# A fused conditioning, expert and adapter kernel on one core: wait order, the adapter-bias product, gathers and the last tile's stores moved

## The chip, the cores and the metric

One core of a Trainium2 chip runs the whole program. The metric is the device time of one execution in microseconds (us), the median over several runs.

## The reference

The input `x` has 128 samples of 32 rows with 256 columns: 4096 tokens of width 256. Each sample has an index `itok` from 0 to 7. What is computed, cut to what matters:

```
w   = L0_cond_weights[itok]                       # a 32x32 mix of each sample's rows
z   = einsum('bct,bcd->bdt', x, w)                # 4096 tokens x 256
logits = z @ Wg + bg; top 2 of 4 experts, softmax over the two
for each expert: the 1024 tokens with the highest score (capacity)
    y = gelu(tok @ W1) @ W2 * p;  out[token] += y
x1  = x + out
gate, up = x1 @ Wg + lora, x1 @ Wu + lora         # lora: rank 16, chosen by itok
h   = silu(gate) * up;  d = h @ Wd + lora
out = x1 + d @ (weight * scale).T + bias
```

## The kernel before, in words

All engines run their own written-out instruction stream and meet in semaphores. Products of f32 data are made of three products of a high and a low part (lines 1429 to 1431, helper `product`): ScalarE (ACT) writes the high part, VectorE (DVE) the difference.

**The head, 0 to 61 us.** TensorE (PE) makes the expert logits; DVE searches each expert's threshold. Meanwhile PE works through 37 items: 32 mix products of tokens (`item`, line 1482), four products that fold the last weight matrix into `Wd` (`fold_half`, L1496), and one, `item(ITEMS - 1)`, that folds it into the adapter matrix (L1485, the bias product of the title); ACT copies each out. The mixed rows go to `flat_rows` in HBM (queue of SyncE, SP). `route_read` (DVE, to L1086) writes the list of token rows of an expert, `slot_row`, and raises `route_out`; GpSimd (POOL) then gathers the rows: `gather(b)` waits and issues four indirect DMAs of 128 rows (L496). Before `gather(0)` POOL waits for `flat_out` and `spare_out`, that is for the rows in HBM.

**Layer 0, 61 to 250 us.** Eight batches `b` of 512 tokens, two for each expert. A step `s` is one slice of 128 hidden units: PE makes the up product of step s, then the down product of step s - 2 (`down`). Batch 0 and batch 7 are cut into two parts of 256 tokens, with eight steps each, so there are 80 steps. The first batch's four chunks of 128 tokens are transposed by PE (`first_transposed`, L1558): chunks 0 and 1 before step 0, chunk 2 after step 1 and chunk 3 after step 2; ACT copies them out (`first_hi`, L624) and DVE makes the low part (`first_lo`, L1096). `slot_scales(0)` (ACT, L635) follows the last chunk, and `gather(1)` waits for it. Between the chunks and step 0, `keep_busy` runs two products without use (L1527). Chunks 2 and 3 are first needed in step 8. Step 0 begins with four products of high parts of the chunks (L1574) and goes on with two of the low parts (L1577).

In the first half the order of PE's stream is: `first_transposed(0)`, `item(ITEMS - 1)`, `first_transposed(1)`, a wait for the copy of that item, `keep_busy`, a wait for the low parts of `w1`, step 0.

**Between the layers, 237 to 263 us.** Layer 1 sorts the samples into eight tiles of 16, each with at most two adapters. POOL's order there is: `scatter(6)`; `gather_b(0)` and `gather_b(1)`, which load the adapter matrices of tiles 0 and 1 (L531, 128 rows of 8 KB each, so 1 MB each); a wait for `ids_in` (from DVE, L1202, the tokens' order) and three more semaphores; four gathers of the first tile's rows (`x1_first`, L561, 128 KB each); a wait until they have landed; `scatter(7)`. PE waits for the four (`first_in`) and transposes them (L1638) between the down products of the last two steps.

**Layer 1, 263 to 587 us.** Eight tiles of 512 tokens in eight steps each. The last tile's output is finished in two halves of 256 tokens: PE ends a half (L1733 to 1735), DVE adds bias and residual with one instruction for each of two column blocks (`finish_last`, L1368), and `last_stores` (L390) writes it: 16 samples, one DMA of 32 KB each, eight on SP's queue and eight on ACT's, four for each half. A store of 32 KB is 256 pieces of 128 bytes (2 blocks x 128 partitions x 32 numbers). Earlier tiles are stored by SP alone (L474).

Of the kernel before, what the change touches and what calls it, by code (L numbers as in the profile page):

```python
# [63 lines left out]
def adaln_moe_lora(nc, A, outT):  # L64
# [11 lines left out]
    with ctx:  # L76
# [247 lines left out]
        out_done = [sem(f"out_done{i}") for i in range(2)]  # L324
# [47 lines left out]
        FIRST_BANKS = (6, 7, 4, 5)  # L372
        LO_W1, LO_ALL = 2 * KD, 2 * KD + 2
# [7 lines left out]
        def last_stores(queue, side):  # L381

            t, n = NB1 - 1, SB // 4
            mine = [[(2 * j + side) * n + i for i in range(n)] for j in range(2)]
            to = [[queue.value_load(sample_at[0:1, t * SB + i:t * SB + i + 1], min_val=0, max_val=TOK // 32 - 1) for i in half]
                  for half in mine]
            for j in range(2):
                queue.wait_ge(out_ev, KD * (NB1 + j))
                for i, s_ in zip(mine[j], to[j]):
                    queue.dma_start(out_v[:, :, bass.ds(s_, 1), :], out_sb[1][:, :, i * 32:(i + 1) * 32].unsqueeze(2)  # L390
                                    ).then_inc(out_done[1], 16)
# [4 lines left out]
        def _(sp):  # L396
# [79 lines left out]
            last_stores(sp, 0)  # L476
            sp.wait_ge(out_done[0], 16 * SB * NB1 // 2)
            sp.wait_ge(out_done[1], 16 * SB * NB1 // 2)

        @block.gpsimd  # L480
        def _(pool):
# [7 lines left out]
            def gather(b):  # L489
                e, half = b // 2, b % 2  # L490
                pool.wait_ge(route_out, e + 1)
                if b:
                    pool.wait_ge(xsT, parts_before(b))
                    pool.wait_ge(slot_in, b)
# [21 lines left out]
            pool.wait_ge(flat_out, 128)  # L516
            pool.wait_ge(spare_out, 32)
# [36 lines left out]
            for t in range(2):  # L554
                gather_b(t)
# [4 lines left out]
            for q in range(GB):  # L560
                pool.indirect_dma_start(  # L561
                    out=x1_first[:, q, :], out_offset=None, in_=x1_rows[:, :],
                    in_offset=bass.IndirectOffsetOnAxis(ap=x1_row[:, q:q + 1], axis=0)).then_inc(first_in, 16)
            pool.wait_ge(first_in, 16 * GB)
# [5 lines left out]
            for t in range(2, NB1):  # L570
                gather_x1(t)
                gather_b(t)
                gather_bd(t)

        @block.scalar
        def _(act):
# [92 lines left out]
            first_hi(0)  # L669
            act.wait_ge(item_mm, ITEMS)  # L670
            act.activation(raw_bd[:, 0, :], bank[(ITEMS - 1) % 4][:, 0:D], ACT.Copy).then_inc(item_ev, 1)
            first_hi(1)
            for s in range(STEPS0):
# [8 lines left out]
                if s in (1, 2):  # L682
                    first_hi(s + 1)
                if s == 2:
# [97 lines left out]
            last_stores(act, 1)  # L782

        @block.vector
        def _(dve):
# [451 lines left out]
            for s in range(STEPS0):  # L1237
# [4 lines left out]
                if s in (1, 2):  # L1242
                    first_lo(s + 1)
# [645 lines left out]
```

## Time and profile before

| | us |
|---|---|
| median of 3 runs | 589.03 (589.01 to 590.47) |
| time of the profiled execution | 588.83 |
| its span | 587.0 |
| PE busy | 562.7 (96%) |
| DVE busy | 372.0 (63%) |
| ACT busy | 242.4 (41%) |
| POOL busy | 142.6 (24%) |

The span runs from the first to the last record of the profile; 1.8 us of the execution's time lie around it. An engine's busy time counts its instructions alone, and the ends of matmuls are modelled.

### The profile page before, as it was taken

To read this page: it belongs to the slowest core of one execution; us is meant where nothing else is said; L and a number is where in the kernel's file an instruction comes from. 1 tells how busy PE (TensorE), PEld (TensorE's weight loads), DVE (VectorE), ACT (ScalarE), POOL (GpSimd) and SP (SyncE) were. 2 spreads that over 40 slices of the span, in tenths; PEclk is the share of its full clock that TensorE was granted. 3 is DMA by queue.
4 is the path that set the end of the run, shared out by engine and by line. 5 is a ranking of instruction groups with operands and counts; after the bars stand their busy time and mean duration, and the time that the engine had idled before them with its cause. 6 is when DMAs were issued, how large, how long until landed. Compare 5 with 4: busy or idle time off the path is not lost.

```text
span 587.0 us, 10367 instructions
## 1 busy us (share of the span) xinstructions
PE 562.7 (96%) x3583; PEld 470.0 (80%) x3583; DVE 372.0 (63%) x901; ACT 242.4 (41%) x545; POOL 142.6 (24%) x122
## 2 busy tenths in 40 slices
PE   4778999999999999999999999999999999999996
PEld 3556899999999999978878878788788788787885
DVE  7989668656776567665574575575665645754733
ACT  2645558747766655653322322324124123123110
POOL 3001402657446442664012030030030030100000
PEclk9999999999999999999999999999999999999999
DMA  8994666884285231732004022041041040120012
GB/s 327 340 358 164 205 237 187 228 186 68 53 229 169 46 46 17 201 54 73 0 10 135 10 93 59 3 129 25 0 135 17 0 141 11 64 59 5 12 26 36
DMA packets 64798, 61.04 MB, mean 104 GB/s; under 512 B 37456, under 2 KB 56656, under 8 KB 63472
## 3 DMA queue, kind: packets, MB, share of 16 engines
q1 hardware_dynamic: 53312, 37.97, 21.3%
q0 software_dynamic: 9264, 22.22, 15.5%
q10 hardware_dynamic: 2176, 0.26, 0.3%
q8 instruction: 25, 0.41, 0.3%
q14 instruction: 21, 0.17, 0.1%
HBM read 45.17 MB, written 19.47 MB: 110 GB/s over the span
## 4 chain that ended last, share of the span: by engine, by line
PE 89%; DVE 5%; DMA 3%; POOL 1%; issue 1%; SPq 0%; ACT 0%; DVEq 0%; POOLq 0%
PE bank L1429 25%; PE bank L1431 24%; PE bank L1430 24%; PE bank L1698 5%; PE bank L1656 3%; DMA xT<-in_xT 1%; DMA x_first<-x_rows,x_row 1%; PE bank L1536 1%; DMA xg<-flat_rows,slot_row 1%; PE bank L1545 1%; PE bank L1648 1%; PE bank L1445 1%; PE bank L1665 1%; PE bank L1666 1%; PE bank L1786 1%
## 5 line engine op out<-in xcount | busy, mean ns | idle before, releaser
L760 ACT ACTIVATE act<-bank 128x512 f32<-128x512 f32 x64 | 38.2, 598 | 183.0 <-PE bank L1698 183.0
L1385 DVE TENSOR_TENSOR prod<-bank,act 128x512 f32<-128x512 f32 x64 | 44.2, 690 | 97.7 <-PE bank L1698 97.3
L1241 DVE TENSOR_TENSOR hid_lo<-hf,hid_hi 128x512 fp32r<-128x512 f32 (+1 forms) x80 | 46.6, 585 | 52.9 <-ACT hf L681 52.4
L1429 PE MATMUL bank<-w_hi,hid_hi 128*128 128x256 f32 x256 | 71.8, 280 | 0.0
L1430 PE MATMUL bank<-w_lo,hid_hi 128*128 128x256 f32 x256 | 71.4, 279 | 0.0
L1431 PE MATMUL bank<-w_hi,hid_lo 128*128 128x256 f32 x256 | 71.3, 279 | 0.0
L678 ACT ACTIVATE hid_hi<-bank 128x512 fp32r<-128x512 f32 (+1 forms) x80 | 41.1, 514 | 64.8 <-PE bank L1431 63.3
L507 POOL DMA_INDIRECT x_rows<-y_sb,slot_row x32 | 52.1, 1628 | 42.5 <-ACT y_sb L648 24.6
L531 POOL DMA_INDIRECT b_pair<-b_rows,b_row x8 | 8.2, 1028 | 200.7 <-PE bank L1746 200.0
L1429 PE MATMUL bank<-xs_hi,w_hi 128*128 128x512 f32 (+1 forms) x158 | 56.5, 357 | 0.0
L1431 PE MATMUL bank<-xs_hi,w_lo 128*128 128x512 f32 (+1 forms) x158 | 55.0, 348 | 0.0
L496 POOL DMA_INDIRECT xg<-flat_rows,slot_row x32 | 35.3, 1103 | 80.4 <-DVE slot_row L1086 33.2
L1430 PE MATMUL bank<-xs_lo,w_hi 128*128 128x512 f32 (+1 forms) x158 | 54.8, 347 | 0.0
L1429 PE MATMUL bank<-hid_hi,wd_hi 128*128 128x512 f32 (+1 forms) x144 | 52.7, 366 | 0.0
L1431 PE MATMUL bank<-hid_hi,wd_lo 128*128 128x512 f32 (+1 forms) x144 | 52.7, 366 | 0.0
L1430 PE MATMUL bank<-hid_lo,wd_hi 128*128 128x512 f32 (+1 forms) x144 | 52.6, 365 | 0.0
L1429 PE MATMUL bank<-x1s_hi,wg_hi 128*128 128x512 f32 x124 | 50.4, 407 | 0.0
L1430 PEld LDWEIGHTS bank<-w_lo,hid_hi 128*128 128x128 f32 x256 | 48.2, 188 | 2.0
L1429 PEld LDWEIGHTS bank<-w_hi,hid_hi 128*128 128x128 f32 x256 | 48.1, 188 | 2.0
L1430 PE MATMUL bank<-x1s_lo,wg_hi 128*128 128x512 f32 x124 | 48.7, 393 | 0.0
L1431 PE MATMUL bank<-x1s_hi,wg_lo 128*128 128x512 f32 x124 | 48.4, 390 | 0.0
L1431 PE MATMUL bank<-x1s_hi,wu_lo 128*128 128x512 f32 x124 | 48.4, 390 | 0.0
(323 smaller groups left out, 1258.6 us busy)
## 6 DMA issues: line engine op xcount, KB each, us to landing
w_raw<-in_L_ffn_W SPq DMA_DIRECT2D x8, 1024.0 KB, 6.9
flat_rows<-x_sb SPq DMA_DIRECT2D x8, 520.0 KB, 5.3
x_sb<-in_x SPq DMA_DIRECT2D x8, 512.0 KB, 8.7
x_rows<-in_x SPq DMA_DIRECT2D x4, 1024.0 KB, 8.6
outT<-out_sb SPq DMA_DIRECT2D x120, 32.0 KB, 1.6
xT<-in_xT SPq DMA_DIRECT2D x3, 1024.0 KB, 7.4
xT<-in_xT SPq DMA_DIRECT2D x2, 512.0 KB, 10.6
wdT<-in_wdT SPq DMA_DIRECT2D x1, 1024.0 KB, 6.0
```

Of the source, the lines that this page charges most:

```text
L496: pool.indirect_dma_start(out=xg[:, q, :], out_offset=None, in_=flat_rows[:, :], in_offset=bass.IndirectOffsetOnAxis(ap=slot_row[:, e, hal ...
L507: pool.indirect_dma_start(out=x1_rows[:, :], out_offset=bass.IndirectOffsetOnAxis(ap=slot_row[:, e, half * GB + q:half * GB + q + 1], axis=0),
L531: pool.indirect_dma_start(out=b_pair[t % 2][:, :].bitcast(f32), out_offset=None, in_=b_rows[:, :], in_offset=bass.IndirectOffsetOnAxis(ap= ...
L678: act.activation(hid[s % 4][0][:, n], bank[s % 2][:, n], ACT.Gelu)
L760: act.activation(act1[h % 2][:, :], bank[h % 2][:, :], ACT.Silu).then_inc(silu1, 1)
L1241: dve.tensor_tensor(lo[:, n], hf[s % 2][:, n], hi[:, n].bitcast(f32), ALU.subtract).then_inc(hid0, 1)
L1385: dve.tensor_tensor(prod[par][h][:, :], bank[2 + h % 2][:, :], act1[h % 2][:, :], ALU.mult).then_inc(prod1, 1)
L1429: pe.matmul(out, lh, rh, start=start, stop=False, skip_group_check=True)
L1430: pe.matmul(out, lh, rl, start=False, stop=False, skip_group_check=True)
L1431: return pe.matmul(out, ll, rh, start=False, stop=stop, skip_group_check=True)
L1656: last = pe.matmul(bank[6][r, :], ad_pair[par][:, h, :], prod[par][h][:, :], start=h < 4, stop=h >= 4, skip_group_check=True, tile_positio ...
L1698: pe.matmul(out[:, :], b_pair[par][:, i * HID + h * P:i * HID + (h + 1) * P], u[:, :], start=False, stop=True, skip_group_check=True).then ...
```

## The change

Five edits:

1. POOL: the waits for `flat_out` and `spare_out` stand inside `gather(0)`, behind the one for `route_out`.
2. PE: `item(ITEMS - 1)` comes ahead of `first_transposed(0)`, and `keep_busy` between `first_transposed(0)` and `first_transposed(1)`, behind a wait for the items up to the last but one. ACT copies that item out ahead of `first_hi(0)`.
3. Chunk 3 is transposed, copied and split after step 3, not after step 2 (`LATE_STEPS`), and `slot_scales(0)` goes with it.
4. POOL: `gather_b(1)` is issued after the four gathers of the first tile's rows.
5. The last tile: samples 6 and 7 are stored by POOL on a semaphore of its own; SP and ACT store seven each. DVE makes the additions of the second half in two lots of 128 tokens (four instructions of 128 columns for two of 256), and each queue waits for the lot it stores. SP waits for POOL's stores too at the end.

```diff
+        LATE_STEPS = (1, 3)
...
-            t, n = NB1 - 1, SB // 4
-            mine = [[(2 * j + side) * n + i for i in range(n)] for j in range(2)]
...
+        LAST_SP, LAST_ACT, LAST_POOL = (0, 1, 2, 8, 9, 12, 13), (3, 4, 5, 10, 11, 14, 15), (6, 7)
+        def last_stores(queue, mine, landed):
+            t, seen = NB1 - 1, None
+            to = [queue.value_load(sample_at[0:1, t * SB + i:t * SB + i + 1], min_val=0, max_val=TOK // 32 - 1) for i in mine]
+            for i, s_ in zip(mine, to):
+                lots = 0 if i < 8 else 1 + (i - 8) // 4
+                if lots != seen:
+                    queue.wait_ge(out_ev, KD * (NB1 + lots))
+                seen = lots
+                queue.dma_start(out_v[:, :, bass.ds(s_, 1), :], out_sb[1][:, :, i * 32:(i + 1) * 32].unsqueeze(2)
+                                ).then_inc(landed, 16)
...
-            last_stores(sp, 0)
+            last_stores(sp, LAST_SP, out_done[1])
             sp.wait_ge(out_done[0], 16 * SB * NB1 // 2)
-            sp.wait_ge(out_done[1], 16 * SB * NB1 // 2)
+            sp.wait_ge(out_done[1], 16 * (SB * NB1 // 2 - len(LAST_POOL)))
+            sp.wait_ge(pool_out, 16 * len(LAST_POOL))
...
             def gather(b):
                 pool.wait_ge(route_out, e + 1)
+                if b == 0:
+                    pool.wait_ge(flat_out, 128)
+                    pool.wait_ge(spare_out, 32)
...
-            pool.wait_ge(flat_out, 128)
-            pool.wait_ge(spare_out, 32)
             gather(0)
...
-            for t in range(2):
-                gather_b(t)
+            gather_b(0)
             pool.wait_ge(ids_in, 4)
...
+            gather_b(1)
             pool.wait_ge(first_in, 16 * GB)
             scatter(NB0 - 1)
...
+            last_stores(pool, LAST_POOL, pool_out)
...
-            first_hi(0)
             act.wait_ge(item_mm, ITEMS)
             act.activation(raw_bd[:, 0, :], bank[(ITEMS - 1) % 4][:, 0:D], ACT.Copy).then_inc(item_ev, 1)
+            first_hi(0)
             first_hi(1)
...
-                if s in (1, 2):
-                    first_hi(s + 1)
-                if s == 2:
+                if s in LATE_STEPS:
+                    first_hi(2 + LATE_STEPS.index(s))
+                if s == LATE_STEPS[1]:
                     slot_scales(0)
...
-                    for k in range(KD):
-                        dve.wait_ge(acc1, NB1 + (KD if j else k))
-                        dve.scalar_tensor_tensor(out_sb[1][:, k, c], last_out(j, k), out_bias[:, k:k + 1],
-                                                 x1T[1][:, k, c], ALU.add, ALU.add).then_inc(out_ev, 1)
+                    for at_ in range(0, BT // 2, P) if j else (0,):
+                        n = P if j else BT // 2
+                        to = slice(c.start + at_, c.start + at_ + n)
+                        for k in range(KD):
+                            dve.wait_ge(acc1, NB1 + (KD if j else k))
+                            dve.scalar_tensor_tensor(out_sb[1][:, k, to], last_out(j, k)[:, at_:at_ + n], out_bias[:, k:k + 1],
+                                                     x1T[1][:, k, to], ALU.add, ALU.add).then_inc(out_ev, 1)
...
+            item(ITEMS - 1)
             first_transposed(0)
-            item(ITEMS - 1)
+            pe.wait_ge(item_ev, ITEMS - 1)
+            keep_busy(WAIT_ROWS, bank[2], w1)
             first_transposed(1)
             pe.wait_ge(item_ev, ITEMS)
-            keep_busy(WAIT_ROWS, bank[2], w1)
             pe.wait_ge(lo0, LO_W1)
```

DVE's `first_lo` and PE's `first_transposed` in the steps are changed to `LATE_STEPS` in the same way as ACT's `first_hi`.

## Rows read from the trace of the kernel before

**Rows 1.** Waits of PE, whole span: total us, times, longest.
```profile
PE bank L1558 <- DMA xg<-flat_rows,slot_row: 1.3, 2, 1.0
PE bank L1638 <- DMA x_first<-x_rows,x_row: 1.2, 1, 1.2
```
**Rows 2.** Timeline of PE, 59 to 78: start, us, instruction [idle before <-releaser].
```profile
59.32 0.33 PE L1558 MATMUL bank<-ident_r,xg 128*128 128x128 f32 x2 [1.05 <-DMA xg<-flat_rows,slot_row]
59.49 1.10 PE L1485 MATMUL bank<-wfT_s,bdT 128*128 128x256 f32 x4
60.53 0.22 PEld L1558 LDWEIGHTS bank<-ident_r,xg 128*128 128x128 f32 x2 [0.35 <-DMA xg<-flat_rows,slot_row]
61.06 0.74 PE L1527 MATMUL bank<-w_hi 128*128 128x512 f32 x2 [0.16 <-ACT raw_bd L671]
...
62.10 0.40 PE L1577 MATMUL bank<-xs_lo,w_hi 128*128 128x256 f32 x2
...
64.65 0.28 PE L1431 MATMUL bank<-w_hi,hid_lo 128*128 128x256 f32 x1
65.14 0.36 PE L1558 MATMUL bank<-ident_r,xg 128*128 128x128 f32 x2 [0.21 <-DMA xg<-flat_rows,slot_row]
...
77.99 0.45 PE L1545 MATMUL bank<-ident_r,xg 128*128 128x128 f32 x4
```
**Rows 3.** Timeline of POOL, 56 to 88, the first gather of three batches.
```profile
56.25 1.14 POOL L496 DMA_INDIRECT xg<-flat_rows,slot_row  x1 [17.52 <-DVE slot_row L1086]
...
66.80 0.95 POOL L496 DMA_INDIRECT xg<-flat_rows,slot_row  x1 [5.09 <-ACT slot_p L635]
...
87.25 1.16 POOL L496 DMA_INDIRECT xg<-flat_rows,slot_row  x1 [15.72 <-DVE slot_row L1086]
```
**Rows 4.** Timeline of DVE, 55 to 87 and 239: the lists' last instructions and two low parts.
```profile
55.21 0.17 DVE L1086 SCALAR_TENSOR_TENSOR slot_row<-route_t 128x8 int32<-128x8 f32 x1
...
59.55 1.21 DVE L1102 TENSOR_TENSOR w_lo<-w_raw,w_hi 128x1024 fp32r<-128x1024 f32 x1
...
61.35 0.42 DVE L1096 TENSOR_TENSOR xs_lo<-bank,xs_hi 128x256 fp32r<-128x256 f32 x1 [0.26 <-ACT xs_hi L624]
...
86.81 0.17 DVE L1086 SCALAR_TENSOR_TENSOR slot_row<-route_t 128x8 int32<-128x8 f32 x1
...
239.11 1.08 DVE L1202 TENSOR_SCALAR x_row<-bank,pack_f 32x32 int32<-32x32 f32 x4
```
**Rows 5.** Timeline of POOL, 237 to 257: an adapter gather, first tile's gathers, last scatter.
```profile
237.54 1.01 POOL L531 DMA_INDIRECT b_pair<-b_rows,b_row  x1 [0.30 <-issue]
...
240.46 0.95 POOL L561 DMA_INDIRECT x_first<-x_rows,x_row  x1 [0.43 <-DVE x_row L1202]
...
244.41 1.55 POOL L561 DMA_INDIRECT x_first<-x_rows,x_row  x1 [0.30 <-issue]
...
256.26 1.56 POOL L507 DMA_INDIRECT x_rows<-y_sb,slot_row  x1 [0.31 <-issue]
```
**Rows 6.** DMA issues in the window 240 to 241: times, median us to landing.
```profile
x_first<-x_rows,x_row POOLq DMA_INDIRECT x1, 6.1
```
**Rows 7.** DMA issues of the whole span: times, median us to landing.
```profile
x_sb<-x_rows,x_row POOLq DMA_INDIRECT x28, 3.1
```
**Rows 8.** Timeline of PE, 250 us: the transposes of the first tile.
```profile
250.44 0.83 PE L1638 MATMUL bank<-ident_r,x_first 128*128 128x128 f32 x8 [1.24 <-DMA x_first<-x_rows,x_row]
```
**Rows 9.** Timeline, 579 to 585: the last additions and the last stores' issues.
```profile
579.83 0.87 DVE L1368 SCALAR_TENSOR_TENSOR out_sb<-bank,pack_f,x1T 128x256 f32<-128x256 f32 x2
...
580.88 4.26 SPq L390 DMA_DIRECT2D outT<-out_sb  x8
...
580.88 4.38 ACTq L390 DMA_DIRECT2D outT<-out_sb  x8
...
582.02 0.88 DVE L1368 SCALAR_TENSOR_TENSOR out_sb<-bank,pack_f,x1T 128x256 f32<-128x256 f32 x2 [1.32 <-PE bank L1735]
```
**Rows 10.** Stretches: us, PE, PEld, DVE, ACT, POOL busy, clock, DMA share, GB/s.
```profile
584.00:585.00 1.00, 0.00 (x0) 0.00 (x0) 0.00 (x0) 0.00 (x0) 0.00 (x0) 0.72 0.88 130
```

More of the change, by code:

```diff
@@ L323, in adaln_moe_lora @@
         acc1, out_ev = sem("acc1"), sem("out_ev")
-        out_done = [sem(f"out_done{i}") for i in range(2)]
+        out_done, pool_out = [sem(f"out_done{i}") for i in range(2)], sem("pool_out")
         b_out, packed_in, placed, ids_mm, ids_in = (sem("b_out"), sem("packed_in"), sem("placed"), sem("ids_mm"),
@@ L379, in adaln_moe_lora @@
         out_v = outT.rearrange("k p (s n) -> p k s n", n=32)
-        def last_stores(queue, side):
-            t, n = NB1 - 1, SB // 4
-            mine = [[(2 * j + side) * n + i for i in range(n)] for j in range(2)]
[L385 to L391, printed above, removed]
+        LAST_SP, LAST_ACT, LAST_POOL = (0, 1, 2, 8, 9, 12, 13), (3, 4, 5, 10, 11, 14, 15), (6, 7)
[9 more added lines that the diff above has]
+                                ).then_inc(landed, 16)
         block = ctx.enter_context(nc.Block())
@@ L781, in _ @@
             steps1(NB1 - 1, 1, False, True)
-            last_stores(act, 1)
+            last_stores(act, LAST_ACT, out_done[1])
         @block.vector
@@ L1241, in _ @@
                 dve.tensor_tensor(lo[:, n], hf[s % 2][:, n], hi[:, n].bitcast(f32), ALU.subtract).then_inc(hid0, 1)
-                if s in (1, 2):
-                    first_lo(s + 1)
+                if s in LATE_STEPS:
+                    first_lo(2 + LATE_STEPS.index(s))
                 if h in (4, 6) and b + 1 < NB0 and (b or part):
@@ L1619, in _ @@
                     down(s - 2)
-                if s in (1, 2):
-                    first_transposed(s + 1)
+                if s in LATE_STEPS:
+                    first_transposed(2 + LATE_STEPS.index(s))
                 if h in (3, 5) and b + 1 < NB0 and (b or part):
```

## The prediction

> **What bounds it now.** The first thing to read is the page's table of busy time: PE is busy for 562.7 of 587.0 us, so only places where PE stands still, and the tail behind its last product, can give time back. The list of PE's waits over the whole span is read next: behind the head (before 50 us) it has three entries with a DMA or a copy behind them, and two of them hold 2.5 us: the transposes of the first batch's chunks (L1558, 1.3 us in two waits) and those of the first tile (L1638, 1.2 us in one) [rows 1]. From 66 to 249 us and from 263 to 581 us PE waits for nothing. The chain of waits passes through both places: `slot_row`, the four POOL gathers, their DMA; and the tokens' order, four POOL gathers, their DMA. The timelines around the two places and around the end then give the terms.
>
> **The change, part by part.** I count against the profiled execution: span 587.0, time 588.83, which is 0.2 under the median of 589.03.
>
> *POOL's wait order (edit 1).* `slot_row` ends at 55.21 + 0.17 = 55.38 and the first gather starts at 56.25, 0.87 later; in batch 2 the same instruction ends at 86.98 and its gather starts at 87.25, 0.27 later [rows 3, 4]. The rows were stored long before, so no DMA explains the difference. What differs is where the wait for the late semaphore stands: third of three, right before the DMA, in batch 0; first of three, with two satisfied waits behind it, in batch 2. The wait for the tokens' order, first of four, also takes 0.27 (239.11 + 1.08 = 240.19, gather at 240.46) [rows 4, 5]. The edit puts `route_out` first. I take 0.27: the gathers start 0.60 earlier. Bounds: 0 (the position was not the reason) and 0.60.
>
> *Item, keep_busy and the copies (edit 2).* PE is idle from 58.27 to 59.32 and waits again before 60.53 [rows 2]. The four products of the bias item run in the first gap: starts are (60.53 - 59.49)/4, at most 0.26, apart, so from 58.27 to about 59.2. Then comes chunk 0, whose rows landed at about 59.3 [rows 2] and now land 0.6 earlier; then `keep_busy`, at most 0.74; then chunk 1 at about 60.1, its rows having landed at 59.93 (60.53 - 0.60). ACT copies the item ahead of chunk 0's copy; before, that copy ended 0.47 behind the item (60.59 to 61.06), so chunk 0 is held up by less than 0.5, and both chunks' high parts are there before 61.0. Behind that DVE is late next: it makes `w_lo` from 59.55 to 60.76, then chunk 0's low part, then chunk 1's. Its last start was 61.35, after ACT; without that wait it follows chunk 0's at 61.02, 0.34 behind it at the earliest, and ends at 61.02 + 0.42 = 61.44 [rows 4]. So the low products of step 0 start at 61.47 in place of 62.10 [rows 2]: 0.63. If edit 1 gives nothing, chunk 1 stays at 60.53, its low part ends at about 61.75, and the gain is 0.33.
>
> *Chunk 3 a step later (edit 3).* The down product before chunk 3 issues its last matmul at 64.65, the next could go at 64.77, and the transposes start at 65.14: 0.37 of waiting for the fourth gather [rows 2]. One step of batch 0 is 1.4 us, and that wait goes. The two transposes themselves (0.2) only move. ACT's and DVE's copies of the chunk move with them and lie beside PE; they are needed in step 8. `slot_scales(0)` moves too, so `gather(1)` starts some 0.5 us later than 66.80 [rows 3]: one step later (+1.4), less the 1.0 that PE is ahead. Its fourth issue is three times 1.25 behind its first, about 71, and lands some 3 to 4 us later, at 75, against its first use at 77.99 - 1.0 = 77.0 [rows 2, 3]. Cost nothing; two microseconds cover it. SP's queue waits for these rows before it loads the second expert's weights, and those are first used in step 16, five steps behind this place.
>
> Head together: 0.63 + 0.37 = **1.00**, between 0.70 and 1.10.
>
> *Gather_b(1) behind the first tile's gathers (edit 4).* POOL is not the gain: the first `x1_first` gather starts 0.27 after the tokens' order and does so still. What goes is 1 MB in front of these gathers in POOL's queue of transfers. The first of them took 6.1 us from issue to landing [rows 6], where gathers of the same size later take 3.1 [rows 7]. The fourth was issued at 244.41 and PE started at 250.44, after 1.24 of waiting, ready at 249.20 [rows 5, 8]. With 3.1, plus 0.6 for its longer issue (1.55 for 0.95), it lands at 248.1, before PE is ready, and all of the wait goes: 1.24. But the last gather of a group has landed late before: the first batch's fourth, issued some 4.5 behind 56.25, held PE until 65.14, 4.3 later, where its first landed in 3.0 [rows 2, 3]. With 4.3 and the 0.6 it lands at 249.3, and 1.1 is left. I take **1.10**. Lower bound 0, if the late landing has nothing to do with the queue. `gather_b(1)` itself (1.0 us and 0.3 between issues) now stands ahead of `scatter(7)`, and its semaphore is used 30 us later. The scatter waits for the landing anyway; its first two rows start no later than before (250.57), its last two wait for ACT, and `gather_x1(1)` behind it has 12 us until its first use.
>
> *The last tile (edit 5).* SP's eight issues take 4.26 us, that is seven spacings of 0.556 and a last issue of some 0.37; it starts at 584.77, ACT's last at about 584.86, and the span ends 2.14 after that [rows 9]. The second half's additions end at 582.02 + 0.88 = 582.90 [rows 9], when the four earlier issues end too: queue and DVE are late together. With the change, three issues end at 582.54 at the queue. DVE's lots: an instruction of 256 columns takes 0.44; one of 128 saves half of its columns, about 0.14, so 0.30, and the first lot is there at 582.62, the second at 583.22 (all four cost 1.2, where two cost 0.88). A queue starts 0.18 after DVE (580.70 and 580.88 in the first half) [rows 9]: 582.80, 583.36, then 583.91, 584.47. The last issue starts **0.30** earlier. Upper bound 0.56: one issue less and no wait for DVE.
>
> POOL's two stores start at about 581.0 (0.27 behind the addition) to 581.5 (0.8). The trace before has no store of this kind from POOL. Lower bound 0.95 an issue, as a gather of 128 rows; upper 3.1, twice a scatter of 128 rows (1.56) [rows 5], for 256 pieces. I take 1.0 to 1.5, nearer the gather, a plain copy without addition: the second issue ends at 583.3 to 584.3 and lands 2.2 later, before SP's and ACT's last, at 586.4. They hide it. That cover ends at 1.9 per issue.
>
> A third queue may also move nothing. While the stores run, the DMA engines are 88% busy at 130 GB/s [rows 10]. If that is the limit, the stores end when they did before, and the tail gives 0 where I take 0.30. The Trainium skill says so (DMA: Bandwidth & Descriptors, "Rules for kernel authors"): spreading DMAs over SP, ACT and GpSimd does not help bandwidth, all run on the same 16 engines, and only issue time is saved. The row does not decide it: at 100% the same bytes would still take some 12% less than the 4.2 us they took.
>
> POOL's first gathers of batches 0 and 2 took 1.14 and 1.16, that of batch 1 0.95, with DVE at work beside the longer ones [rows 3]. The Trainium skill (SBUF — State Buffer, "Who interferes with whom") has it that a DVE instruction in a 2-port mode, or with two SBUF inputs, shuts GpSimd out until it ends. By that rule gathers that start 0.6 earlier fall beside other DVE instructions, and one may take up to 0.5 more or less; chunk 1 has half a microsecond of slack against DVE's low parts.
>
> **Sum.** 1.00 + 1.10 + 0.30 = 2.40: span 584.6, profiled time 586.4, median 589.03 - 2.40 = **586.6**. Behind each place PE has no wait for 180 and 320 us, so what is won stays won.
>
> **Rivals.**
> - *The wait's position is not the reason* and the landing tail stays: head 0.70, first tile 0 to 0.5, tail 0.3, so 1.0 to 1.5: 587.5 to 588.0. For it: only one pair of rows with the same instruction. Against: the third case, the tokens' order. Chance 0.18.
> - *The DMA engines bound the last stores*: tail 0, total 2.1: 586.9. Chance 0.15.
> - *POOL's stores come last, slower than before.* Place: behind 580.7 on POOL. Price P for each: the second lands at 581.0 + 2P + 0.3 + 2.2 = 583.5 + 2P, and the other queues' last at 586.4. At 1.9 (twice a gather) it lands at 587.3, 0.6 after the old landing at about 586.7; the total is 1.5: 587.5. At 3.1 it lands at 589.7; 3.0 lost less 2.1 won: 589.9, slower. The sign turns at P = 2.65. For it: 256 pieces, and POOL's work is by row. Against: a gather of 8 KB rows takes POOL 1.01, hardly more than one of 1 KB (0.95) [rows 5]. Chance 0.12 for 1.9 and about, 0.05 for over 2.65.
> - *A gain is given back*, by batch 1's rows or the second expert's weights being late at 77 to 90 us, up to 1.0: 587.6. Two microseconds of slack are against it. Chance 0.05.
>
> That leaves 0.45 for the forecast, 586.6, whose own range is 586.0 to 587.1 (head 0.9 to 1.1, first tile 0.95 to 1.24, tail 0.1 to 0.56). The range for 8 in 10 reaches to the rivals on the fast side of no change and takes in the upper bounds: 585.8 to 588.2.
>
> A measurement of this kernel can tell about 0.3%, 1.8 us, from no change, which puts the line at 587.26. Below it lie the forecast, the engine-bound rival and a little of the others: 0.66. Between: the wait rival, POOL at 1.9, given back: 0.29. Slower by over 0.3% needs POOL's stores above 3.5 us each or something unseen: 0.05.
>
> **What would show it.** The first gather starts 0.27 after `slot_row`; the wait for chunk 3 is gone and step 4 is 1.0 earlier; `x1_first`'s first gather lands in about 4 us, not 6.1, and PE's wait at L1638 is under 0.3; the last issues of SP and ACT start some 2.4 us earlier than 584.8 and POOL's second store lands before theirs. I am wrong if POOL still takes 0.87, if L1638 still waits a microsecond, or if the chain's end is a POOL store.

## The result, and the profile after

The changed kernel takes 593.07 us (median of six executions, 591.80 to 594.13) where the kernel before takes 589.09 beside it: a ratio of 1.0066, 95% interval 1.0050 to 1.0082. It is **slower by 4.0 us**; the prediction was 586.6, faster by 2.4.

The profiled execution took 593.32, its span is 591.6, 4.6 over the 587.0 of before. The page's head, chain and busy times:

```profile
span 591.6 us, 10371 instructions
PE 564.7 (95%) x3583; PEld 472.1 (80%) x3583; DVE 372.7 (63%) x903; ACT 242.0 (41%) x545; POOL 143.1 (24%) x124
PE 90%; DVE 5%; DMA 2%; issue 1%; ACT 0%; SPq 0%; POOL 0%; POOLq 0%; ACTq 0%; DVEq 0%
```

PE's work is no less, and the chain no longer goes through gathers (DMA 2% for 3%). The list of PE's waits, those behind 56 us, answers to [rows 1] (line numbers moved with the edits: L1567 is the L1558 of before, the transposes of the first batch's chunks):

```profile
PE bank L1438 <- ACT hf L687: 1.2, 1, 1.2
...
PE bank L1567 <- DMA xg<-flat_rows,slot_row: 0.7, 1, 0.7
PE bank L1584 <- ACT xs_hi L630: 0.6, 1, 0.6
...
PE bank L1438 <- DVE hid_lo L1247: 0.3, 1, 0.3
```

The wait for `x_first` is gone, as forecast. In its place stands one of the same size for ACT, a little earlier in time. The timeline of POOL after (for [rows 3] and [rows 5]) shows the edits doing what they say:

```profile
57.69 1.18 POOL L503 DMA_INDIRECT xg<-flat_rows,slot_row  x1 [18.91 <-DVE slot_row L1092]
59.16 1.50 POOL L503 DMA_INDIRECT xg<-flat_rows,slot_row  x1 [0.30 <-issue]
...
242.07 0.97 POOL L565 DMA_INDIRECT x_first<-x_rows,x_row  x1 [1.90 <-DVE x_row L1208]
...
247.54 0.94 POOL L536 DMA_INDIRECT b_pair<-b_rows,b_row  x1 [0.30 <-issue]
```

`slot_row` ends at 57.40 here, so the gather follows it by 0.29, where it was 0.87. But the second gather takes 1.50; in the kernel before it took 0.97:

```profile
57.70 0.97 POOL L496 DMA_INDIRECT xg<-flat_rows,slot_row  x1 [0.30 <-issue]
```

The end of the run is where the time is. Three views of after: POOL's timeline, the engines' last instructions (source line L76, the closing of the block; columns: shortest, median and longest duration in ns, then the first and the last start in us), and SP's waits.

```profile
584.38 1.52 POOL L393 DMA_DIRECT2D outT<-out_sb  x2 [69.56 <-issue]
```

```profile
L76 POOLq DRAIN  x1: 6405/6405/6405, 585.0 to 585.0; - x1
L76 ACTq DRAIN  x1: 150/150/150, 587.3 to 587.3; - x1
L76 SPq COMPARE_BRANCH  x1: 41/41/41, 589.0 to 589.0; - x1
L76 SPq EVENT_SEMAPHORE  x1: 17/17/17, 591.5 to 591.5; - x1
```

```profile
SPq L76 <- PEq L76: 2.3, 1, 2.3
```

All stores have landed and SP is through its waits at 589.0. DRAIN is the instruction with which each engine closes its stream. POOL's runs from 585.0 to 591.4, and the program ends 0.2 behind it. (The wait is written down as one for PE's sequencer, but PE had long been done; the row to read is the DRAIN.) In the kernel before the same instruction was out of sight in the middle of the last tiles, behind POOL's last DMA:

```profile
511.60 0.95 POOL L539 DMA_INDIRECT bd_pair<-bd_rows,bd_row  x1 [0.30 <-issue]
```

```profile
L76 POOLq DRAIN  x1: 12964/12964/12964, 508.9 to 508.9; - x1
L76 SPq COMPARE_BRANCH  x1: 41/41/41, 586.6 to 586.6; - x1
```

It ended at 521.8 there, 9.3 after that DMA's issue had ended, and nobody waited for it.

**Four distances.** To compare executions I cut each span at three events: `slot_row`'s end; the start of step 0's low products (62.10 in [rows 2]); the end of PE's last product; the end of the span. For after against before they give

| | before | after | difference |
|---|---|---|---|
| start to `slot_row` | 55.38 | 57.40 | +2.02 |
| to step 0's low products | 6.72 | 6.57 | -0.15 |
| to the end of the last product | 519.89 | 520.29 | +0.40 |
| to the end of the span | 5.01 | 7.34 | +2.33 |
| sum | 587.0 | 591.6 | +4.60 |

The first line lies wholly ahead of the change. PE's sixteen logit products took 2.02 us before and 3.42 after, and the stretches 16:20 and 20:24 (columns as in [rows 10]) say why. Before, then after:

```profile
16.00:20.00 4.00, 2.59 (x28) 2.06 (x18) 3.36 (x12) 2.65 (x4) 1.03 (x1) 1.00 1.09 353
20.00:24.00 4.00, 3.15 (x15) 2.72 (x15) 3.76 (x29) 3.33 (x9) 0.00 (x0) 1.00 1.09 353
```

```profile
16.00:20.00 4.00, 2.59 (x28) 1.96 (x27) 3.57 (x12) 2.10 (x3) 1.04 (x1) 0.88 1.09 353
20.00:24.00 4.00, 4.00 (x19) 3.73 (x19) 1.89 (x14) 2.93 (x7) 0.00 (x0) 0.70 1.09 352
```

The granted clock was full, 2.4 GHz, throughout before, and for a part of these 8 us at its lower level, 1.2 GHz, in after. PE had been busy for all of 12:16 in after (4.00) and for 3.92 of it in before.

### The profile page after: what moved, and what is told of

It reads as the page before. It is cut to its first block, busy times and chain, and to the rows that moved or that the text cites. A ratio compares the mean times of both kernels' runs of the same rounds, so it can differ in the third digit from the quotient of the medians.

```text
span 591.6 us, 10371 instructions
## 1 busy us (share of the span) xinstructions
PE 564.7 (95%) x3583; PEld 472.1 (80%) x3583; DVE 372.7 (63%) x903; ACT 242.0 (41%) x545; POOL 143.1 (24%) x124
## 4 chain that ended last, share of the span: by engine, by line
PE 90%; DVE 5%; DMA 2%; issue 1%; ACT 0%; SPq 0%; POOL 0%; POOLq 0%; ACTq 0%; DVEq 0%
PE bank L1438 25%; PE bank L1440 24%; PE bank L1439 24%; PE bank L1708 5%; PE bank L1666 3%; DMA xT<-in_xT 1%; DVE passed L887 1%; PE bank L1454 1%; PE bank L1545 1%; PE bank L1554 1%; PE bank L1658 1%; PE bank L1675 1%; PE bank L1676 1%; PE bank L1796 1%; PE bank L1517 1%
```

## The experiments

Theory A: POOL's DRAIN behind its late stores makes the tail 2.3 longer. Rivals: B, the stores' landing or the smaller lots of the last additions; C, the middle (ACT's stand-still) belongs to edit 4; D, the late `slot_row` belongs to the edits. The kernel before was timed beside all of them, and each ratio is against it.

### 1. The last tile alone, and the change without POOL's stores

`b_only_tail` is the kernel before with edit 5. `a_no_pool_stores` is the kernel after with this edit, cut (SP's waits at the end are changed to match):

```diff
-LAST_SP, LAST_ACT, LAST_POOL = (0, 1, 2, 8, 9, 12, 13), (3, 4, 5, 10, 11, 14, 15), (6, 7)
+LAST_SP, LAST_ACT = (0, 1, 2, 3, 8, 9, 12, 13), (4, 5, 6, 7, 10, 11, 14, 15)
...
-            last_stores(pool, LAST_POOL, pool_out)
```

> The kernel before with edit 5 alone (the last tile: POOL stores two samples, seven each on SP and ACT, last additions in two lots). Theory A, from the trace after: two DMAs late on POOL's queue put POOL's closing DRAIN behind them, and it ends about 5.5 us after the last of them is issued, where SP's own end would come 0.3 earlier than before or at the same time. So this kernel is 2.0 to 2.6 us slower than before (about 591.3), with the chain ending in POOL's DRAIN near the span's end. Rival B, the prediction's own step: the tail gives 0 to 0.3 (588.7 to 589.1), and the time of after is lost in the head and the middle. Head and middle (to 580 us) should stand within 0.5 us of the kernel before by either.

> The kernel after, but POOL stores nothing and SP and ACT have eight stores each again (the two lots of the last additions stay). Theory A: 2.3 us less than after, 590.8. Rival B (the lots, or the landing of the stores, hold the end): within 0.5 us of after.

Measured: `b_only_tail` 592.05, ratio 1.0061 (1.0044 to 1.0079); `a_no_pool_stores` 587.21, ratio 0.9987 (0.9973 to 1.0000), both beside 588.53. The last product ends at 581.95 in the first and at 580.99 in the second; their spans, 589.3 and 586.0, end 7.35 and 5.01 behind it. Theory A stands, and the lots of the last additions are worth nothing: 5.01 with them, 5.01 without. The second kernel came out 3.6 under the expected 590.8, which had been counted from 593.07, the first measurement of after; section 5 shows what else was in that one. The chain of `b_only_tail` is as follows (start, us, what):

```profile
580.82 1.24 issue
582.05 0.04 POOLq L392
582.10 0.06 POOL outT L392
582.16 0.52 issue
582.67 0.93 POOLq L76
```

```profile
L76 POOLq DRAIN  x1: 6402/6402/6402, 582.7 to 582.7; - x1
L76 ACTq DRAIN  x1: 150/150/150, 585.0 to 585.0; - x1
L76 SPq COMPARE_BRANCH  x1: 41/41/41, 586.7 to 586.7; - x1
```

The seven stores did what was forecast for the issue and nothing for the end. SP's issues end at 584.80 (580.84 + 3.96), 0.34 before the 585.14 of [rows 9], with the last product at the same time (581.95 against 581.99). SP is through its waits at 586.7; before, at 586.6. The DMA engines' busy share falls to 0.27 in the half microsecond from 585.95, after 0.97 and 0.95 in the two ahead of it; in the kernel before it falls to 0.15 in that from 585.99. The same bytes end at the same time.

The median is 3.5 over before, though, not 2.3. Experiment 3 finds 0.45 of the rest.

### 2. One store of POOL, early or late, and stores out of the way

`b_pool_one_first_half` and `b_pool_one_second_half` are the kernel before, with POOL taking sample 7, or sample 15, from ACT (cut; the line for sample 15 has `NB1 + 1`, and SP's waits at the end are changed to match):

```diff
...
+            pool.wait_ge(out_ev, KD * (NB1 + 0))
+            pool.dma_start(out_v[:, :, bass.ds(s_, 1), :], out_sb[1][:, :, i * 32:(i + 1) * 32].unsqueeze(2)).then_inc(pool_out, 16)
```

`b_pool_stores_tile6` is the kernel before with two stores on POOL, samples 6 and 7 of the last tile but one (tile 6), taken from SP.

> The kernel before, but POOL stores one sample of the last tile, in its first half (one for the two of edit 5; ACT has seven, SP eight). Theory A1 (DRAIN ends a fixed 5.5 us after POOL's last issue has ended): the store is issued at about 582.1 to 582.9, DRAIN ends at 588.4, the span is 1.4 over that of before. Theory A2 (DRAIN is a fixed 6.4 us from where it starts): it starts at about 582.2, ends at 588.6, and the span is 1.6 over. Rival B (nothing of DRAIN depends on the stores): no change.

> The kernel before, but POOL stores one sample of the last tile's second half (sample 15, from ACT). Theory A: the store can be issued 2.2 later than in the first half; it took 1.4 from the addition's end to its start and 0.78 itself, and DRAIN ended 5.4 after it in three profiles. The second half's additions end 0.9 after PE's last product and a bit, so DRAIN ends at 0.95 + 1.4 + 0.8 + 5.4 = 8.6 behind PE's last product, where the kernel before ends 5.0 behind it: 3.6 slower (about 592.1). A rival in which late stores cost by their landing alone (2.2 to 2.4 after the issue): 0 to 0.6 slower.

> The kernel before, but POOL stores two samples of tile 6, some 25 us before the end, in place of SP. Theory A (only the place of POOL's last DMA counts, its DRAIN needs 5 to 6 us after it and is hidden here): the time of before within 0.3, DRAIN over by 570 us. Rival E (the mere use of direct stores on POOL costs something, in the code of POOL or in its first gathers, whose first took 1.17 to 1.18 in both profiles with such stores and 1.14 in all four without): 0.5 to 1.2 slower than before, with the first gather at 1.17 and the second at 1.48.

| | ratio (interval) | span's end behind the last product |
|---|---|---|
| one store, first half | 1.0034 (1.0020 to 1.0048) | 6.50 |
| one store, second half | 1.0077 (1.0052 to 1.0101) | 8.69 |
| two stores, tile 6 | 1.0007 (0.9990 to 1.0023) | 5.05 |

POOL's stores and DRAIN, first of the second-half kernel, then of the tile-6 kernel:

```profile
583.71 0.78 POOL L580 DMA_DIRECT2D outT<-out_sb  x1 [71.75 <-issue]
```

```profile
L76 POOLq DRAIN  x1: 6193/6193/6193, 583.7 to 583.7; - x1
L76 SPq COMPARE_BRANCH  x1: 41/41/41, 586.2 to 586.2; - x1
```

```profile
553.13 1.52 POOL L581 DMA_DIRECT2D outT<-out_sb  x2 [39.93 <-issue]
```

```profile
L76 POOLq DRAIN  x1: 6402/6402/6402, 553.7 to 553.7; - x1
```

The later store moves the end with it: it starts 2.30 behind the last product, where the early one starts 0.12 behind, and the ends are 2.19 apart. SP is ready 3.7 before DRAIN is over. DRAIN ended at 589.3 for an issue that ended at 583.9 (583.12 + 0.78), 589.9 for 584.5, 560.1 for 554.65, and 589.1 for 583.60 in `b_only_tail`: **5.4 to 5.5 us behind the end of POOL's last direct issue**, whether one or two (the other five kernels or repeats with such stores give the same), and out of sight where 27 us follow. One store less saved 0.85 (7.35 to 6.50), one issue. That is theory A1; A2's fixed 6.4 fails, as DRAIN took 6.19 with one store and 6.40 with two. The tail of the first-half kernel is 1.5 longer than before's and its median 2.1 over, again more than the tail.

### 3. What direct stores on POOL do to the head

All kernels with a direct store on POOL, tile 6 among them, have another head: rival E had forecast gathers of 1.17 and 1.48 for the tile-6 kernel, and they took 1.17 and 1.48, while its 0.5 in the time lies within the interval. The gathers of the first batch in the tile-6 kernel with edits 1 to 4 (`edits_1_to_4_pool_tile6`), and those of edits 1 to 3 alone:

```profile
57.59 1.17 POOL L503 DMA_INDIRECT xg<-flat_rows,slot_row  x1 [19.33 <-DVE slot_row L1097]
59.06 1.50 POOL L503 DMA_INDIRECT xg<-flat_rows,slot_row  x1 [0.30 <-issue]
```

```profile
56.12 1.14 POOL L500 DMA_INDIRECT xg<-flat_rows,slot_row  x1 [17.53 <-DVE slot_row L1088]
57.57 0.97 POOL L500 DMA_INDIRECT xg<-flat_rows,slot_row  x1 [0.30 <-issue]
```

> Edits 1 to 4, the last tile as before, and POOL stores two samples of tile 6. Theory F (any direct store on POOL makes its first gathers slower, also here): gathers of 1.17, 1.5, 1.45, low products of step 0 at 6.6 after slot_row in place of 6.12, end of the span 5.0 behind PE's last product, DRAIN hidden; the time 0.5 over edits 1 to 4. Theory G (the slower gathers belong to the place of the stores at the end): 6.12 and the time of edits 1 to 4.

Measured: 590.90, ratio 1.0016 (0.9998 to 1.0034), beside 1.0010 for edits 1 to 4 in the same measurement; low products of step 0 at 6.55, the tail 5.07, DRAIN hidden. That is theory F in the trace; a time difference of 0.4 is within the intervals. Over all twenty traces, the second gather took 1.47 to 1.50 in the ten with a direct store on POOL and 0.97 in the ten without. Step 0's low products, measured from `slot_row`:

| | without a direct store on POOL | with |
|---|---|---|
| no edit in the head | 6.72, 6.76, 6.76 | 7.24, 7.18, 7.11, 7.19 |
| edits 1 to 3 | 6.12, 6.12, 6.12, 6.11, 6.11 | 6.57, 6.66, 6.59, 6.55, 6.59, 6.55 |

So edits 1 to 3 give 0.6 in either column, and the stores take 0.45 back, 520 us before they run. The first gather is 0.03 longer there, and the second then lies otherwise against DVE's four `w_lo` instructions beside it. That this shift makes the step of 0.5 is likely (gathers took 0.95 to 0.97, 1.43 to 1.50 or 1.98 to 2.02 in this place, in jumps of half a microsecond) but wasn't tried. For it speaks that in the ten traces with such stores a `w_lo` instruction had begun 0.05 to 0.09 ahead of the second gather and took 0.68 to 0.69, while in the ten without it had begun 0.02 to 0.04 ahead and took 0.74 to 0.77, and the gather was the short one. Why the first gather is longer is open.

### 4. The head's edits, together and apart

> The kernel before with edits 1 to 3 alone. Theory D1: the 2.0 us by which slot_row comes later after the change is the state of that one execution's clock (granted clock .88 to .90 at 15 to 30 us), not the edits, so this kernel is 0.4 (what the trace after shows between slot_row and 80 us) to 1.0 (the prediction) faster than before, and slot_row ends at about 55.4. Theory D2: the edits shift the code so that the head is slower whenever they are in: slot_row ends near 57.4 and the time is 1.0 to 1.6 over before (590.1 to 590.7).

> The kernel before with edit 1 alone (POOL waits for route_out first). The prediction's step: the first gather starts 0.27 to 0.29 after slot_row where it was 0.87, so chunk 0 comes 0.60 earlier, and the low products of step 0, 6.72 after slot_row before, come 0.2 to 0.6 earlier. Rival (the place of the wait is nothing, the three edits of the head work only together): the gather stays at 0.87 and step 0 at 6.7. In the time at most 0.6 either way, which three rounds can't tell from nothing; the trace tells it.

> The kernel before with edit 2 alone (the bias item ahead of chunk 0, keep_busy ahead of chunk 1). The prediction gives 0.33 where edit 1 gives nothing: the first gather at 0.87 after slot_row, the low products of step 0 at 6.4 after it. Rival: PE only waits elsewhere, 6.7. Edits 1 and 2 with 3 gave 6.12.

| | ratio (interval) | first gather after `slot_row` | low products of step 0 after `slot_row` |
|---|---|---|---|
| edits 1 to 3 | 0.9985 (0.9973 to 0.9998) | 0.29 | 6.12 |
| edit 1 | 0.9992 (0.9979 to 1.0005) | 0.28 | 6.20 |
| edit 2 | 1.0016 (1.0001 to 1.0031) | 0.88 | 6.67 |

Edit 1 alone is 0.52 of the 0.60. Edit 2 alone is 0.05, where 0.33 was expected; its time lies just above that of before, which its trace doesn't explain. Its timeline of PE, and that of edits 1 to 3:

```profile
60.73 0.37 PE L1558 MATMUL bank<-ident_r,xg 128*128 128x128 f32 x2 [0.42 <-DMA xg<-flat_rows,slot_row]
```

```profile
59.56 0.69 PE L1529 MATMUL bank<-w_hi 128*128 128x512 f32 x2
60.38 0.36 PE L1560 MATMUL bank<-ident_r,xg 128*128 128x128 f32 x2
61.31 0.35 PE L1577 MATMUL bank<-xs_hi,w_hi 128*128 128x256 f32 x1 [0.56 <-DVE w_lo L1104]
...
61.95 0.50 PE L1580 MATMUL bank<-xs_lo,w_hi 128*128 128x256 f32 x2
```

With edit 2 alone chunk 1's rows land when they did before, PE waits 0.42 for them, and the copy behind them, which `keep_busy` used to cover, is a wait of 0.56. From chunk 1's transposes to the first high product it is 0.93 in both (61.31 less 60.38; the first high product of edit 2 is at 61.66); before it was 1.10.

Theory D1 holds: `slot_row` ended at 55.83 with edits 1 to 3 and at 57.06 with edit 4 alone, whose head is the code of before, with a granted clock of 0.86 and 0.71 in the two stretches. It is the execution's clock.

### 5. Edit 4, and two kinds of measurement

> The kernel before with edit 4 alone (the second gather of adapter matrices behind the first tile's gathers). Theory C1: the wait of 1.24 before the transposes of the first tile goes, and the 2.2 us in which ACT stood still at 247 to 249 us in the trace after belongs to that execution or to the shifted stream, so this kernel is 1.0 to 1.2 faster than before (588.0). Theory C2: the edit itself makes ACT stand still (the gather of adapter matrices moved beside it), so PE's wait changes its place and the time is that of before or up to 0.7 above (589.1 to 589.8).

> The kernel after, unchanged, once more. The trace after shows 2.3 us lost at the end, slot_row 2.0 late and ACT standing still for 2.2 us at 247 to 249 us. Theory A+random: only the 2.3 is there in every execution; in this profile PE's last product to the end of the span is 7.3 again, while ACT's gap before hid_hi near 249 is 0.7 to 1.0 and slot_row ends anywhere from 55.4 to 57.4; the median is 589.5 to 591.5. Theory S (the change as a whole makes the head late and ACT stand still each time): slot_row again near 57.4, the gap again 2.2, and the median again near 593, 5 over the kernel without POOL's stores.

> The kernel after, unchanged, a third time. It was 1.0066 of before in its first six executions and 1.0029 in the next twelve, beside a kernel before that moved by 0.6 only. Theory J (what came on top of the 2.3 at the end, ACT's stand-still near 248 and the late slot_row, belongs to single executions or to one loading of the program): ratio 1.002 to 1.004, hid_hi's gap near 249 at 0.7 to 1.0, PE's last product 517.9 to 518.1 after step 0's low products. Theory S (it comes back in a part of the executions of this kernel whatever the chip): a ratio near 1.006 again, or executions of both kinds within the twelve.

> The kernel after, unchanged, a fourth time. Theory J (what was on top in the first six executions, ACT's stand-still of 2.2 near 248 us among it, belongs to that loading): 1.002 to 1.005 of before, tail 7.3, PE's last product 517.9 to 518.1 after the low products of step 0. Theory S: 1.006 or more, or PE's last product over 520 after step 0.

Edit 4 alone: 588.68, ratio 1.0001 (0.9990 to 1.0013), no gain. That is theory C2's time without its mechanism, as ACT stands still for 0.7 only in this trace. Yet the trace shows the edit at work: `x_first`'s first gather lands in 2.9 us (6.1 in [rows 6]), PE doesn't wait before the transposes, and the last product comes 518.04 after step 0, 1.85 less than in before.

The kernel after had five measurements. The distance is that from step 0's low products to the end of the last product; the gap is the longest time ACT stood still before `hid_hi` at 246 to 251 us:

| | this / before | ratio (interval) | distance | gap |
|---|---|---|---|---|
| after | 593.07 / 589.09 | 1.0066 (1.0050 to 1.0082) | 520.29 | 2.23 |
| after_again | 590.13 / 588.53 | 1.0029 (1.0017 to 1.0041) | 517.93 | 0.73 |
| after_third | 590.68 / 588.28 | 1.0042 (1.0026 to 1.0058) | 517.95 | 0.72 |
| after_fourth | 593.58 / 590.45 | 1.0060 (1.0036 to 1.0084) | 521.07 | 2.30 |
| after_fifth | 594.68 / 590.15 | 1.0068 (1.0049 to 1.0086) | 521.16 | 2.30 |

The tail was 7.31 to 7.35 in all five. What differs is ACT. The `hid_hi` rows in its timeline, of after and of after_again:

```profile
246.37 0.39 ACT L684 ACTIVATE hid_hi<-bank 128x256 fp32r<-128x256 f32 x1 [0.96 <-PE bank L1440]
...
249.26 0.38 ACT L684 ACTIVATE hid_hi<-bank 128x256 fp32r<-128x256 f32 x1 [2.23 <-PE bank L1440]
```

```profile
246.94 0.38 ACT L684 ACTIVATE hid_hi<-bank 128x256 fp32r<-128x256 f32 x1 [0.73 <-PE bank L1440]
...
249.73 0.38 ACT L684 ACTIVATE hid_hi<-bank 128x256 fp32r<-128x256 f32 x1 [0.71 <-PE bank L1440]
```

By PE's rows the product that the second copy of after reads ended at 248.06 (247.78 + 0.28), 1.2 before the copy started, and PE then stood still for 1.22. In the first measurement of after and in the last two the stand-still is there, in the other two it isn't. Theory J was half right: it doesn't belong to single executions, it comes with the measurement. Theory S is wrong, as two measurements don't have it. A chip of the same number gave one measurement of each kind (after_third, after_fifth), so it isn't simply the chip.

Two more kernels ran beside `after_fourth`: edits 1 to 4 and the change without POOL's stores, each for the second time.

> The kernel before with edits 1 to 4 and the last tile as before. If the lots and the seven stores give nothing (the two profiles with them end 5.0 after PE's last product, as before does), this is the same as the kernel after without POOL's stores: 587.2, 1.3 under before. If the lots help, it is 0.3 above that; if they cost, 0.3 below.

> Edits 1 to 4 once more (0.9990 of before the first time). From the traces: 0.6 at step 0, 0 to 0.3 at chunk 3, and the wait before the first tile's transposes, which was 1.24, 1.16, 1.21 and 0.40 in the four traces without edit 4 and without POOL's stores: together 1.0 to 2.1, so a ratio of 0.9965 to 0.9983. If PE's clock in the head takes it back on average, 0.999 again.

> The kernel after without POOL's stores once more (0.9987 of before the first time). If the lots of the last additions and the order of the stores give nothing, the same as edits 1 to 4 beside it, within 0.4; if they give the 0.30 of the prediction, that much less, which these rounds can't tell from nothing. The tail behind PE's last product is 5.0 either way by the traces so far.

| | first time: ratio, distance | second time: ratio, distance |
|---|---|---|
| edits 1 to 4 | 0.9990 (0.9978 to 1.0002), 518.06 | 1.0010 (0.9996 to 1.0023), 521.48 |
| after without POOL's stores | 0.9987 (0.9973 to 1.0000), 518.04 | 1.0007 (0.9990 to 1.0024), 522.05 |

All four traces of the second measurement have the gap (2.27 to 2.30). There the two kernels' last product comes 3.4 and 4.0 later after step 0 (0.7 of it is another wait for ACT, near 75 us), and what they win elsewhere is gone: `e14_again` came out at 1.0010 where at most 0.9990 was expected. Beside them after was 593.58, 3.2 over the same kernel without POOL's stores, of which the traces show some 2.3 in the tail and 0.44 at step 0 (6.55 to 6.11).

The last pair asked whether the kernel before has the stand-still too.

> The kernel before, unchanged, with a profile of its own. If the kernel after, run beside it, shows ACT's stand-still of 2.2 near 249 us: by theory K (it belongs to the chip) it is here too, and PE's last product comes over 520 us after the low products of step 0; by theory L (edit 4 brings it on such chips) it is not, and the 1.2 of waiting before the first tile's transposes is. If after shows no stand-still on this chip: the wait before the first tile's transposes is 0.4 to 1.24 as in the four traces without edit 4 and without direct stores on POOL, and the low products of step 0 come 6.7 after slot_row.

> The kernel after, unchanged, as the marker of the chip: the tail 7.3 behind PE's last product and the low products of step 0 at 6.6 after slot_row whatever the chip; ratio 1.003 to 1.004 where ACT's gap near 249 us is 0.7, 1.006 where it is 2.2.

`after_fifth` shows it (2.30). `before_again`, beside it, shows a smaller one:

```profile
246.81 0.38 ACT L678 ACTIVATE hid_hi<-bank 128x256 fp32r<-128x256 f32 x1 [1.44 <-PE bank L1431]
```

Its distance is 519.65. In the other measurements the kernels without edit 4 and without direct stores had 519.89, 519.32, 519.36 and 518.76, waits of 1.24, 1.16, 1.21 and 0.40 before the transposes among it; here there is no such wait. So on such a measurement the kernel before loses about what it would have waited anyway, while kernels with edit 4 go from 518.0 to 520.3 to 522.1: neither K nor L alone. The median of before, though, was 589.09, 590.45 and 590.15 in the three measurements with the gap and 588.53, 588.53 and 588.28 in the three without; its one trace there doesn't show where that is lost. I can't tell what holds ACT. In the six traces with a gap of 2.2 or more, a packet of the instruction queue q8 began 0.3 to 0.9 us before the gap's end:

```profile
q8 instruction: 1, 0.02, 11.5%
```

(after, window 248.5 to 249.0; the gap ends at 249.26). Such a packet runs there in the other traces as well, without a gap, no row ties q8 to ACT, and the packet took 0.92 (11.5% of 16 engines for 0.5 us), so it was still under way when ACT went on; it was in the other five too. So this is a weak suspicion. What does go with the gap is an 8 KB packet of the other instruction queue, q14: it came 3.1 to 3.2 behind the gap's end in the six, and 0.2 to 1.2 ahead of the same copy in the thirteen traces in which ACT stood still for 0.7. Whether it is a cause or a consequence isn't shown. The Trainium skill (Runtime: NRT & Kernel Launch, "Instruction fetch mechanics") has each engine fetch its instructions in blocks of 16 KiB by a DMA queue of its own; the packet's 0.02 MB fits one block, and no run here took that transfer away.

## Why the prediction was wrong

**The step that failed is edit 5's, "They hide it".** I followed POOL's two stores to their landing, ahead of 586.4, and no further. Each issue took 0.76 (two in 1.52), less than my 1.0 to 1.5 and far from the 2.65 at which I had the sign turn. The first started 1.40 behind its additions (580.68 to 582.08 in the trace of the tail alone), where I had 0.3 to 0.8. The landing was indeed hidden. What I didn't count is that an engine also has to close: POOL's DRAIN ends 5.4 to 5.5 behind its last direct issue. The term of +0.30 measured -2.3 in the tail and -0.45 in the head, 3.1 off in all, and that alone turns the forecast's -2.4 into +0.7, about half of the way to the measured +4.0. "Slower by over 0.3%" had a chance of 0.05, for very slow stores "or something unseen"; it was the latter, and the chain's end runs through POOL's store and DRAIN, the last of the signs of being wrong. The row was there to be read: the DRAIN of before, 13 us long, ending 9.3 behind POOL's last DMA.

**The rival with the right sign had the wrong price.** "POOL's stores come last" named the place and the side, and gave it 0.05 because it priced the issue alone. Its formula was also misread: 583.5 + 2P reaches the cover's 586.4 at P = 1.45, not at 1.9. With 0.76 to 0.78 an issue that made no difference.

**The rest of edit 5.** The last issue of SP ended 0.34 earlier (0.30 predicted), and the landing did not: the rival of the bound DMA engines was right. The Trainium skill's rule that spreading DMAs over the issuing engines saves issue time and no bandwidth (DMA: Bandwidth & Descriptors, "Rules for kernel authors") is what the runs show: SP through at 586.7 for 586.6. The lots alone did nothing, since a queue with eight stores is behind the additions anyway.

**Edit 1 was right.** The position of the wait gives 0.59 (0.87 to 0.28). Its share at step 0 alone is 0.52.

**Edit 2 was right in the sum and wrong in the parts.** 0.60 for the 0.63 predicted, but edit 2 alone gives 0.05 for my 0.33. I had looked only at DVE's low part, 1.24 behind chunk 1's transposes; PE's own way is longer, 0.93 for the copy and 0.55 for the four high products, with nothing between the transposes and the first of them now. The gathers' 0.5 more beside other DVE instructions, which I had as a possibility with half a microsecond of slack, is what happened in after, and the slack was not there. The rule of the Trainium skill that I weighed there (SBUF — State Buffer, "Who interferes with whom") has a DVE instruction with two SBUF inputs contend only with a GpSimd instruction that reads SBUF, a condition that I left out. The long gathers (1.50 for 0.97) do lie beside such instructions of DVE, `w_lo`'s; the short ones do too, and no run here shows that the port is the reason.

**Edit 3** was to give 0.37, read from one execution. Of the nine traces without the edit only three have that wait (0.21, 0.30, 0.33). In traces without the gap the distance to the last product is 517.93 to 518.06 with edits 3 and 4 and 518.04 with edit 4 alone, so nothing. With neither, and POOL's direct stores, it is 518.05, 518.28, 518.65 and 518.83, and the last two have a third wait for the first batch's rows: the term is 0 to 0.8 and depends on how late these are.

**Edit 4 was right on its mechanism and mis-sized.** PE waits in none of the eleven traces with it. But 1.24 was one execution: of the other eight traces without the edit three wait (1.16, 1.21 and 0.40), and four with POOL's direct stores and `before_again` don't. And the median gave nothing at all. Two things stand against it: ACT's gap, in three of six measurements, which takes 2.3 or more from the kernels with the edit, and the end of `slot_row`. It lay between 55.4 and 58.3 in the twenty traces, at 57.2 on average in the eleven with edit 4 and at 56.3 in the nine without, with no edit in that code. A part of this is the clock: in ten traces the granted clock was below full between 16 and 24 us, and `slot_row` ended at 57.06 to 58.31; in the other ten it was full there, and the ends are 55.37 to 57.05. Seven of the eleven are of the first kind and three of the nine, and with 1.4 between the means of the two kinds that makes 0.4 of the 0.9. Whether this is chance, and what the rest is, stays open.

**Added up** for a measurement without the gap: -0.60 + 0.45 at step 0, 0 to -1.2 before the first tile, +2.33 in the tail: 1.0 to 2.2 over before, for a measured 1.6 and 2.4 (`after_again`, `after_third`). With the gap: -0.15 and +2.33 again, and 0.6 to 1.5 between the distances of after (520.3 to 521.2) and of `before_again` (519.65): 2.8 to 3.7, for a measured 3.1 to 4.5, so up to 0.8 is open. `b_only_tail`'s 3.5, of which head and tail explain 2.8 at most, stays with 0.7 open.

**No version beats before by what can be told.** Edits 1 to 3 alone are the best seen, 0.9985 (0.9973 to 0.9998), in one measurement; with edit 4 it was 0.9990 and 0.9987, and 1.0010 and 1.0007 the second time.

## What to carry to other kernels

Before an idle queue is given late work, look at how its engine closes: the DRAIN row of before tells the order of what it takes behind that engine's last DMA (9.3 there behind a gather, 5.4 to 5.5 behind a direct store), and it is free only while something longer follows. GpSimd's last DMA belongs so far ahead of the end that its closing fits. A wait of a microsecond read from one execution is a term with a range down to 0, so read the same place in several traces before it becomes a sum's largest term; and a kernel is timed in more than one measurement, with the old one beside it, before a change of 0.2% is believed.

## What the runs showed of the hardware

- POOL's closing DRAIN ends 5.4 to 5.5 us behind the end of its last direct issue (ten traces), 8.9 to 9.3 behind that of its last indirect one (the other ten; 9.3 in before).
- A direct store of 32 KB in 256 pieces took POOL 0.76 to 0.78, and started 1.4 behind the addition it waited for (ten traces); SP and ACT started 0.18 behind theirs (before).
- A kernel with such a store, in the last tile or in tile 6, has a first gather of 1.16 to 1.18 in the head (1.14 without) and a second of 1.47 to 1.50 (0.97 without), half a millisecond before the store.
- A semaphore wait right ahead of an indirect DMA on POOL costs 0.6 more than the same wait two satisfied waits earlier (0.87 to 0.28), with nothing else moved.
- ACT stood still for 2.2 to 2.3 us near 249 us in all kernels with edit 4 in three measurements, and in none in the three others; the cause is open.
